# Reordering the value products of an attention kernel: low halves first, high halves last

## The reference

```
w = softmax(q k^T / 64 + causal mask)
w = w * mask;  w = w / (sum(w) + 1e-8)
out = einsum('bhqk,bhkd->bhqd', w, v)      # the value products
x = x + out @ Wo
```

## Time and profile before

| | |
|---|---|
| median of 3 runs | 3317.49 us |
| profiled execution, its own time | 3318.04 us |
| its span | 3316.3 us |
| granted TensorE clock, mean | 0.987 |
| busy: PE / PEld / DVE / ACT / POOL | 3150.5 / 2412.3 / 2717.3 / 2460.8 / 1551.5 us |
| float32 transposes of L1500 | 4608, 802.0 us |
| high value matmuls, low value matmuls (L1516) | 4608 each, 610.8 and 568.2 us |

### The profile page before, as it was taken

How to read it: one execution, slowest core, us unless ns; L and a number is a source line. 1 busy time by engine, 2 the same in 40 slices (tenths; PEclk the granted TensorE clock), 3 DMA queues, 4 the chain that set the end, 5 groups by cost and what they waited for, 6 DMA issues and landing times.

```text
span 3316.3 us, 77709 instructions
## 1 busy us (share of the span) xinstructions
PE 3150.5 (95%) x28915; PEld 2412.3 (73%) x28915; DVE 2717.3 (82%) x5085; ACT 2460.8 (74%) x4837; POOL 1551.5 (47%) x1873
## 2 busy tenths in 40 slices
PE   4999997999999999999999999999999999799998
PEld 2677775777777777777777777777777777477776
DVE  7999995877877877787787778778777777799997
ACT  4787764777777777778777777777777777677775
POOL 3344432454455555455445545545545545333333
PEclk9999998999999999999999999999999999899999
DMA  3133313222322233222222223223222323111111
GB/s 112 39 93 87 115 40 89 52 59 67 91 57 70 65 84 72 67 78 66 60 81 74 68 65 82 70 53 96 72 55 52 100 58 102 32 52 58 58 58 39
DMA packets 160357, 231.36 MB, mean 70 GB/s; under 512 B 30064, under 2 KB 72176, under 8 KB 159984
## 3 DMA queue, kind: packets, MB, share of 16 engines
q1 hardware_dynamic: 159984, 226.38, 25.2%
HBM read 93.27 MB, written 32.38 MB: 38 GB/s over the span
## 4 chain that ended last, share of the span: by engine, by line
PE 69%; issue 6%; DVE 5%; ACT 2%; POOL 2%; DVEq 0%; ACTq 0%; POOLq 0%
PE at_t_ps L1500 14%; PE at_o_ps L1516 10%; PE at_side_ps L1414 10%; PE ffn_gu_ps L520 7%; PE at_s_ps L1489 6%; PE at_s_ps L1490 6%; PE at_side_ps L1467 4%; PE at_side_ps L1426 4%; PE ffn_down_ps L545 4%; DVE at_e_rows L1682 2%; PE at_side_ps L1455 2%; ACT at_eT_hi L1598 1%; PE ffn_hT_ps L485 1%; DVE at_eT_lo L1688 1%; DVE at_v_masked L1660 1%
## 5 line engine op out<-in xcount | busy, mean ns | idle before, releaser
L1688 DVE SCALAR_TENSOR_TENSOR at_eT_lo<-at_t_ps,at_eT_hi 128x512 f16<-128x512 f32 (+3 forms) x1536 | 853.2, 556 | 472.3 <-ACT at_eT_hi L1598 446.1
L1590 ACT ACTIVATE at_e_rows<-at_e_rows,at_neg_max 128x1024 f32<-128x1024 f32 (+7 forms) x1024 | 792.2, 774 | 214.1 <-DVE at_neg_max L1682 212.6
L1598 ACT ACTIVATE at_eT_hi<-at_t_ps 128x512 f16<-128x512 f32 (+3 forms) x1536 | 745.2, 485 | 191.3 <-PE at_t_ps L1500 182.4
L1682 DVE CUSTOM_DVE_ANT_0 at_e_rows<-at_s_ps,at_strip,keep_s_scale 128x1024 f32<-128x1024 f32 (+7 forms) x1024 | 828.0, 809 | 9.7 <-PE at_s_ps L1490 6.8
L1500 PE MATMUL at_t_ps<-at_ident,at_e_rows 128*128 128x128 f32 x4608 | 802.0, 285 | 0.1
L1516 PE MATMUL at_o_ps<-at_v_cols,at_eT_hi 128*128 128x132 f16 x4608 | 610.8, 221 | 11.0 <-ACT at_o_raw L1609 6.5
L1516 PE MATMUL at_o_ps<-at_v_cols,at_eT_lo 128*128 128x66 f16 x4608 | 568.2, 193 | 0.0
L1489 PE MATMUL at_s_ps<-at_kh_st,at_q_st 128*128 128x512 f16 (+3 forms) x1536 | 501.8, 327 | 17.9 <-DVE at_acc L1672 12.5
L1516 PEld LDWEIGHTS at_o_ps<-at_v_cols,at_eT_hi 128*128 128x128 f16 x4608 | 433.3, 97 | 91.4 <-DVE at_eT_lo L1688 23.9
L1500 PEld LDWEIGHTS at_t_ps<-at_ident,at_e_rows 128*128 128x128 f32 x4608 | 493.7, 141 | 3.9 <-issue 0.5
L1490 PE MATMUL at_s_ps<-at_kl_st,at_q_st 128*128 128x512 f16 (+3 forms) x1536 | 481.6, 327 | 0.0
(11 more groups left out here) (252 smaller groups left out, 6659.2 us busy)
## 6 DMA issues: line engine op xcount, KB each, us to landing
at_kh_st<-at_k_hi SPq DMA_DIRECT2D x256, 128.0 KB, 2.3
at_kl_st<-at_k_lo SPq DMA_DIRECT2D x256, 128.0 KB, 2.3
at_w_qk<-w_qk_split SPq DMA_DIRECT2D x65, 256.0 KB, 3.0
at_q_st<-at_q_hi SPq DMA_DIRECT2D x128, 128.0 KB, 2.4
at_q_st<-at_q_lo SPq DMA_DIRECT2D x128, 128.0 KB, 2.4
at_w_v<-w_v_split SPq DMA_DIRECT2D x66, 128.0 KB, 2.3
ffn_x_rows<-in_L_attn_query_dram SPq DMA_DIRECT2D x32, 256.0 KB, 3.2
ffn_x_res<-in_L_attn_query_dram SPq DMA_DIRECT2D x32, 256.0 KB, 3.8
```

Of the source, the lines that this page charges most:

```text
L1590: nc.scalar.activation(e_rows[:, n % 4, :w], e_rows[:, n % 4, :w], ACT.Exp, bias=neg_max[:, n % 4:n % 4 + 1], scale=-1.0).then_inc(sem("ex ...
L1598: nc.scalar.activation(eT[0][:, i % EBUF, :count * P], t_ps[i % TBUF][:, :count * P], ACT.Copy, scale=PSCALE).then_inc(sem("eT_hi"), 1)
L1682: nc.vector.tensor_tensor_reduce(e_rows[:, n % 4, :w], s_ps[n % 2][:, col:col + w], strip[:, SEQ - w:], keep["s_scale"][:, 0:1], BIGGEST, ...
L1688: nc.vector.scalar_tensor_tensor(out=eT[1][:, i % EBUF, :count * P], in0=t_ps[i % TBUF][:, :count * P], scalar=PSCALE, in1=eT[0][:, i % EB ...
```

## The change

Inside a group the matmuls are issued in another order. If the group holds the unit's first block, that block's high half still comes first and has start set. Then come the low halves of all blocks of the group, then the remaining high halves. A group that doesn't begin a unit has all its low halves first and then all its high halves. Matmuls, weights, columns, waits and the signal are the same in number and kind; stop goes to the last matmul of the unit's last group. With a and b standing for high and low, a group of four was a0 b0 a1 b1 a2 b2 a3 b3 and becomes a0 b0 b1 b2 b3 a1 a2 a3, or b0 b1 b2 b3 a0 a1 a2 a3 where it doesn't begin a unit. A unit's single first block stays a0 b0.

```diff
@@ def value(i, g, par)
-                for b in range(count):
-                    for s in range(2):
-                        last = nc.tensor.matmul(o[:, :VPART[s]], eT[s][:, i % EBUF, b * P:(b + 1) * P], v_cols[par][:, k0 + b, a, :VPART[s]],
-                                                start=k0 + b == 0 and s == 0, stop=k0 + b == j and s == 1)
+                first = [(0, 0)] if k0 == 0 else []
+                low = [(1, b) for b in range(count)]
+                high = [(0, b) for b in range(len(first), count)]
+                passes = first + low + high
+                for n, (s, b) in enumerate(passes):
+                    last = nc.tensor.matmul(o[:, :VPART[s]], eT[s][:, i % EBUF, b * P:(b + 1) * P], v_cols[par][:, k0 + b, a, :VPART[s]],
+                                            start=k0 + b == 0 and s == 0, stop=k0 + count > j and n == len(passes) - 1)
                 last.then_inc(sem("value_done"), 1)
```

## The result

The changed kernel takes 3292.32 us, the median of 4 runs (3290.27 to 3293.23), against 3317.35 for the kernel before (4 runs, 3316.22 to 3319.31): a ratio of 0.9923 with a 95% interval of 0.9906 to 0.9940. That is 25 us less. The profiled execution took 3293.23 us with a span of 3291.4.

A forecast was written before the change was run, and what follows sets the result against it. TensorE's nearly gapless matmul stream in attention was taken as the bound. A saving of 36.8 us less 10.6 handed back gives 26.2, hence 3291 us; own range 3279 to 3308, upper end carried to 3312.

The forecast's parts named there:

- Step 1: Transpose behind a value group: a high matmul last hides more of its float32 load, saving 28.0 ns per group.
- Step 2: Value groups: one more float16 load falls behind a low matmul and comes late, costing 1.8 ns per group.
- The rival of 44 ns per low matmul: Low matmuls in a row are held by their loads, 44 instead of 31.1 ns: 3331 us, chance 0.09.
- The sum on TensorE: Attention's value groups: 1405 groups times (28.0 - 1.8) ns saved, 36.8 us in all.
- What is handed back: TensorE's waits before the Wo product, v projection and value groups take back 10.6 us of the gain.
- The engines' rival: Attention's exchange with ScalarE and VectorE sets the pace, so TensorE only waits more: 3317 us, chance 0.06.

The follow-up runs named there:

- wide_low: Kernel before, with only the last low matmul of each group over 132 columns instead of 66: 3318.19 us, ratio 1.0000.
- narrow_high: Changed kernel, with the last high matmul of each group over 66 columns instead of 132: 3290.71 us, ratio 0.9919.
- inside: Kernel before, with the new order only in groups 5 to 11 of each pair: 3318.35 us, ratio 0.9999.
- outside: Kernel before, with the new order in all groups of a pair except 5 to 11: 3299.27 us, ratio 0.9944.

## Why the prediction was right, point by point

- **The time.** 3291 forecast, 3292.3 measured, inside the forecast's own range.
- **Step 1, the float32 load under the last matmul.** Right in cause, by wide_low and narrow_high, and in size. Four transposes behind a high matmul were to take 443 ns and take 443.4. The saving is 26.2 ns where four transposes follow and 28.1 where a single one does; I had 28.0. The recorded durations fell as said, the mean of L1500 from 285 to 276 ns.
- **Step 2, float16 loads under low matmuls.** The cost of 1.8 ns per group was too high. A run of four lows ahead of a high averages 121.4 ns (735 runs), which is 30.4 each, against my 31.1; runs of three and two take 92.4 and 63.6. Against a mean of 29.3 that is 4 to 5 ns of lateness for each run of two or more lows, and the high behind it is no longer late (57.5 ns), where the alternating order had 1.8 for each of count - 1 loads. As a mean over the 22 groups of a pair the difference is near 0.1 ns per group. The rival of 44 ns per low matmul is refuted.
- **The sum on TensorE.** About 26.6 (between the two savings) - 0.1 = 26.5 ns in 1405 groups, 37.2 us, against 36.8. The two small errors cancel.
- **What is handed back.** 10.6 us forecast; 37.2 - 25.0 = 12.2 by the times, 11.7 by the windows. The sum came near partly by luck, for its two terms were wrong in opposite directions. A pair with the Wo product went from 35.04 to 34.57 us and one with the v projection from 34.83 to 34.55 (medians). TensorE's stream gains 22 x 26.5 ns = 0.58 us in each, so about 0.12 and 0.30 us are handed back, where I had 0.18 and 0.15. In the first, the origin was misread: the last event that waited for TensorE is not the copy of `at_raw_k` but ScalarE's wait at 1499.82, with five runs behind it and not seven; 5 x 26 = 0.13 us. The run inside agrees: its pair with the Wo product is 0.05 us shorter, what the two other runs gain. In the second I had a guess in place of an origin; the largest loss is the wait of group 20 for its exponential, and the wait ahead of L1426 stayed at 10.1 us when ScalarE was relieved. I also wrote that the waits ahead of L1467 and L1426 would grow to about 42 us; they are at 35.1, and the rest shows as waits for the low half and for the exponential. That what is gained outside is kept was wrong by about 5 us.
- **The engines' rival.** The share of an engine in the stage, 78%, was a poor argument against it. In the stretch that decides it is 90%, and from 1499.82 to the Wo product the rival holds: 5.53 us before, 5.54 after.

## What to carry to other kernels

In a stream of matmuls that each load new weights, read the distances between starts by what ran before, and put the widest matmul last ahead of a slow load: here a float32 load of 128x128 needs about twice the cover of a float16 one (61 against 31 ns, both estimates from these distances), and the reordering cost nothing that the runs show. A gain on the busiest engine counts only outside the stretches where another engine's queue sets the pace; find these by the stretches that keep their length, not by the wait table, whose largest entry moved from one place to another at about the same time (3294.4 against 3292.3 us). Look for the origin of such a stretch in the wait lines of the other engines, to the last one that names TensorE. This schedule, with one output bank and a lag of three groups, stands close to an edge: one group more of lag cost 97 us against the changed kernel.

## What the runs showed of the hardware that was not expected

A matmul of 128x132 in place of 128x66 cost nothing where it stood ahead of a float32 load (wide_low, ratio 1.0000), and one of 66 in place of 132 gained nothing measurable (narrow_high, 3290.71 against 3292.32 us). The lateness of float16 loads under 66-column matmuls was 4 to 5 ns per run of two to four and did not add up with its length (63.6, 92.4 and 121.4 ns).
